# A four-layer graph network: attention scores as eight more columns of the dense product, a closed layer's bias and Relu on turned rows, and the zero fill told between its issues

## The reference, cut to what matters

```python
for l in range(3):
    h = (x @ W[l]).reshape(N, 4, 24)
    alpha_s = einsum('nhc,hc->nh', h, a_src[l])
    alpha_d = einsum('nhc,hc->nh', h, a_dst[l])
    e = leaky_relu(alpha_s[src] + alpha_d[dst], 0.2)
    ex = exp(e - segment_max(e, dst)[dst])
    alpha = ex / (segment_sum(ex, dst)[dst] + 1e-16)
    out = segment_sum(h[src] * alpha[:, :, None], dst)
    x = relu(out.reshape(N, 96) + b[l])
```

## Time and profile before

| | |
|---|---|
| timed runs | 12480.21 us median of 3 (12470.48 to 12484.04) |
| profiled execution | 12461.23 us, span 12459.3 us |
| busy share of the span | PE 49%, DVE 41%, ACT 33%, POOL 63% |
| chain that ended last | POOL 60%, issue 21%, PE 10%, DVE 5% |
| mean granted TensorE clock | 0.641 of full speed |

### The profile page before, as it was taken

How to read it: one execution, slowest core, us unless ns; L and a number is a source line. 1 busy time by engine, 2 the same in 40 slices (tenths; PEclk the granted TensorE clock), 3 DMA queues, 4 the chain that set the end, 5 groups by cost and what they waited for, 6 DMA issues and landing times.

```text
span 12459.3 us, 138299 instructions
## 1 busy us (share of the span) xinstructions
PE 6083.9 (49%) x36087; PEld 5305.1 (43%) x36087; DVE 5101.1 (41%) x15841; ACT 4053.9 (33%) x10426; POOL 7908.1 (63%) x8254
## 2 busy tenths in 40 slices
PE   0288721345555567998344444434343443434443
PEld 0188621234444446776333333434343343433343
DVE  8555400032332233223444444544444454444445
ACT  0199400034444440000333333233333323333332
POOL 1877777557777750000677777567777756777775
PEclk8556765666666668999555555555555555555555
DMA  8144421122222215665222222222222222222222
GB/s 281 24 103 102 134 73 42 55 50 53 53 53 53 53 36 160 215 214 189 69 69 67 68 67 68 53 69 69 67 68 67 68 53 70 68 67 68 67 69 59
DMA packets 1052646, 1038.35 MB, mean 83 GB/s; under 512 B 641642, under 2 KB 758166, under 8 KB 1051952
## 3 DMA queue, kind: packets, MB, share of 16 engines
q1 hardware_dynamic: 704544, 611.05, 16.7%
q0 software_dynamic: 263776, 336.86, 12.3%
q10 hardware_dynamic: 83664, 82.78, 2.0%
HBM read 935.12 MB, written 96.55 MB: 83 GB/s over the span
## 4 chain that ended last, share of the span: by engine, by line
POOL 60%; issue 21%; PE 10%; DVE 5%; ACTq 2%; DMA 1%; ACT 1%; DVEq 0%; POOLq 0%; SPq 0%; PEldq 0%
POOL sb_HG L571 47%; POOL edge_counts L624 13%; PE sums L968 3%; ACTq L642 2%; PE sums L905 1%; PE psA L968 1%; PE psB L968 1%; PE psC L968 1%; PE psD L968 1%; DVE sb_ACC L1939 1%; DMA edge_counts<-sb_HG 0%; PE psD L889 0%; DMA sb_HG<-attention_table,sb_NOW 0%; ACT sb_H L685 0%; PE psA L856 0%
## 5 line engine op out<-in xcount | busy, mean ns | idle before, releaser
L571 POOL DMA_INDIRECT sb_HG<-attention_table,sb_NOW x4980 | 4725.5, 949 | 3087.1 <-DVE sb_NOW L1768 1570.6
L905 PE MATMUL sums<-sb_HG 128*128 128x100 f32 x9984 | 2061.0, 398 | 444.2 <-ACT sb_HG L689 427.1
L905 PEld LDWEIGHTS sums<-sb_HG 128*128 128x128 f32 x9984 | 2028.1, 312 | 454.2 <-ACT sb_HG L689 436.1
L624 POOL DMA_INDIRECT edge_counts<-sb_HG x1625 | 1632.1, 1004 | 743.3 <-issue 489.2
L685 ACT ACTIVATE sb_H<-sb_iota_row,sb_H 128x128 f32<-128x128 f32 x6656 | 2029.1, 387 | 140.3 <-PE sums L905 65.7
L571 POOL DMA_INDIRECT sb_HG<-feature_table,sb_NOW x1612 | 1522.0, 944 | 641.8 <-issue 490.8
L1939 DVE TENSOR_TENSOR sb_ACC<-sb_ACC,sums 128x100 f32 x4992 | 1274.9, 255 | 1146.4 <-PE sums L905 618.9
L915 PEld LDWEIGHTS sums<-sb_HG 128*128 128x128 f32 x6656 | 1300.2, 294 | 345.9 <-issue 345.7
L915 PE MATMUL sums<-sb_HG 128*128 x6656 | 1314.9, 379 | 175.8 <-DVE sb_ACC L1485 80.7
L754 ACT ACTIVATE psC<-sb_SB 128x128 f32<-128x128 f32 x156 | 43.8, 281 | 3922.5 <-DVE sb_SB L1892 3922.5
L1485 DVE TENSOR_TENSOR sb_ACC<-sb_ACC,sums 128x97 f32 (+1 forms) x3328 | 848.7, 255 | 606.2 <-PE sums L915 124.6
(11 more groups left out here) (447 smaller groups left out, 8859.8 us busy)
## 6 DMA issues: line engine op xcount, KB each, us to landing
sb_HG<-edge_counts SPq DMA_DIRECT2D x1152, 256.0 KB, 3.2
sb_H<-rel_rows SPq DMA_DIRECT2D x312, 512.0 KB
sb_HG<-attention_table,sb_NOW POOLq DMA_INDIRECT x4980
sb_HG<-in_edge_attr_dram SPq DMA_DIRECT2D x201, 384.0 KB, 3.6
edge_counts<-sb_LW ACTq DMA_DIRECT2D x12, 6272.0 KB, 42.4
edge_counts<-sb_HG POOLq DMA_INDIRECT x1625
sb_HG<-feature_table,sb_NOW POOLq DMA_INDIRECT x1612, 2.4
sb_EA<-in_edge_attr_dram SPq DMA_DIRECT2D x201, 128.0 KB, 2.5
```

The costliest lines, as they stand in the source:

```text
L571: pool.indirect_dma_start(to, None, rows, bass.IndirectOffsetOnAxis(ap=index, axis=0)).then_inc(landed, 16)
L624: pool.indirect_dma_start(every_count, bass.IndirectOffsetOnAxis(ap=slot_of[:, f:f + 1], axis=0), tally[:, f:f + 1], None).then_inc(scatte ...
L905: last = nc.tensor.matmul(bank[:, k // 4, k % 4 * width:(k % 4 + 1) * width], HOT[:, hot, k, :], G[:, slot, k, 0:width], start=True, stop= ...
```

## The change

Three things change.

1. The fills. ScalarE waits for the fill two back, and tells it, between one issue and the next, instead of telling all after the last issue.
2. The scores. A product of h with a fixed vector is x times a column: W[:, head] times that vector. VectorE makes these columns once in the setup, 4 for the source and 4 for the target, behind each layer's weights in a new tile `WG` of 104 columns. The dense product is then 104 columns wide and gives features and both scores at once. `attend_to` becomes two copies: 100 columns into `ACC` and 4 into `DD`.
3. The close of layers 0 and 1. The division by the sum of weights moves into the next `gat` stage as `prepare` (`divide`, one group at a time, in `ACC`). TensorE turns `ACC` instead of `H`. ScalarE's lift adds the bias, now one value a partition, and rectifies. The last layer's close stays, behind the loop.

```diff
-            for g in [NG - 1, *range(NG - 1)]:
+            FILL = [NG - 1, *range(NG - 1)]
+            def tell_filled(n):
+                act.wait_ge(zeroed[FILL[n]], 16)
+                act.sem_inc(filled, 1)
+            for n, g in enumerate(FILL):
                 width = WIDE if g < NG - 1 else 2 * P
                 act.dma_start(counts[g, :, 0:NB, 0:width],
                               zeros[:, 0:width].unsqueeze(1).broadcast_to([P, NB, width])).then_inc(zeroed[g], 16)
-            for g in [NG - 1, *range(NG - 1)]:
-                act.wait_ge(zeroed[g], 16)
-                act.sem_inc(filled, 1)
+                if n >= 2:
+                    tell_filled(n - 2)
+            tell_filled(NG - 2)
+            tell_filled(NG - 1)
...
-            def lift(t):
+            def lift(t, bias=None):
+                how = {} if bias is None else {"bias": BCOL[:, bias:bias + 1]}
...
-                    nc.scalar.activation(zT[0:D, half, :], psA[0:D, :], ACT.Copy).then_inc(SEM["lifted"], 1)
+                    nc.scalar.activation(zT[0:D, half, :], psA[0:D, :], ACT.Copy if bias is None else ACT.Relu, **how)\
+                      .then_inc(SEM["lifted"], 1)
...
-                lift(Stage(f"gat{l}"))
+                lift(Stage(f"gat{l}"), bias=2 + l if l else None)
...
-                dense_stage(Stage(f"gat{l}"), H, W_GAT + l)
+                dense_stage(Stage(f"gat{l}"), ACC if l else H, WG[:, l, :], WT + HEADS)
...
+            dve.wait_ge(weights_in, (8 + P // DE) * 16)
+            for l in range(LAYERS):
+                for n, r in enumerate((R_ASRC, R_ADST)):
+                    link(v.tensor_tensor(SB[0:D, 0:D], WG[:, l, 0:D], ROWS[0:D, r + l, :], ALU.mult))
+                    link(v.tensor_reduce(WG[:, l, D + n * HEADS:D + (n + 1) * HEADS],
+                                         SB[0:D, 0:D].rearrange("p (h c) -> p h c", h=HEADS), AX.X, ALU.add))
             normalise()
...
-                    dve.wait_ge(SEM["taken"], g + score.base["taken"])
-                    v.tensor_copy(ACC[:, part, 0:D], p)
-                    for n, r in enumerate((R_ASRC, R_ADST)):
-                        last = v.tensor_tensor(by_head[n], p, row(r + l).broadcast_to([P, Q, D]), ALU.mult)
-                    last.then_inc(SEM["scored"], 1)
-                    dve.wait_ge(SEM["scored"], g + (score.base["scored"] + 1))
-                    for n, to in enumerate((ACC[:, part, D:WT], DD[:, part, :])):
-                        last = v.tensor_reduce(to, by_head[n].rearrange("p b (h c) -> p b h c", h=HEADS), AX.X, ALU.add)
-                    return last
-                take(score, attend_to)
+                    v.tensor_copy(ACC[:, part, :], p[:, :, 0:WT])
+                    return v.tensor_copy(DD[:, part, :], p[:, :, WT:WT + HEADS])
+                def divide(g):
+                    part = ACC[:, Q * g:Q * g + Q, 0:D].rearrange("p b (h c) -> p b h c", h=HEADS)
+                    by = ACC[:, Q * g:Q * g + Q, D:WT].unsqueeze(3).broadcast_to([P, Q, HEADS, C])
+                    return v.tensor_tensor(part, part, by, ALU.mult)
+                take(score, attend_to, prepare=divide if l else None, width=WT + HEADS)
...
                 link(v.reciprocal(ACC[:, :, D:WT], ACC[:, :, D:WT]))
-                for h in range(HEADS):
-                    part = ACC[:, :, h * C:(h + 1) * C]
-                    link(v.tensor_tensor(part, part, ACC[:, :, D + h:D + h + 1].broadcast_to([P, NBP, C]), ALU.mult))
-                link(v.tensor_tensor(ACCF, ACCF, over_blocks(row(R_GATB + l)), ALU.add))
-                if l < LAYERS - 1:
-                    link(v.tensor_scalar(H[:, :, :], ACCF, 0.0, None, ALU.max))
+            for h in range(HEADS):
+                part = ACC[:, :, h * C:(h + 1) * C]
+                link(v.tensor_tensor(part, part, ACC[:, :, D + h:D + h + 1].broadcast_to([P, NBP, C]), ALU.mult))
+            link(v.tensor_tensor(ACCF, ACCF, over_blocks(row(R_GATB + LAYERS - 1)), ALU.add))
```

More of the change, by code:

```diff
@@ L133, in gnn_kernel @@
         ones = sb("ones", [P, P])
-        WTS = sb("WTS", [D, 14, D])
+        WTS = sb("WTS", [D, 11, D])
+        WG = sb("WG", [D, LAYERS, WT + HEADS])
         WE = sb("WE", [P, P // DE, D])
         ROWS = sb("ROWS", [P, 7 + 4 * LAYERS, D])
-        BCOL = sb("BCOL", [D, 3])
+        BCOL = sb("BCOL", [D, 3 + LAYERS - 1])
         DD = sb("DD", [P, NBP, HEADS])
@@ L236, in gnn_kernel @@
         W_L0A, W_L0B, W_L0C, W_L0D, W_L11, W_L12, W_IN, W_GCN, W_OUT = 0, 1, 2, 3, 4, 5, 6, 7, 10
-        W_GAT = 11
         TURNED = [W_IN, W_GCN, W_GCN + 1, W_GCN + 2, W_OUT]
@@ L275, in gnn_kernel @@
                  "virtual_made",
-                 "prepared", "flipped", "lifted", "hid_product", "hid_ready", "made", "taken", "scored", "hop_step", "part_step"]
+                 "prepared", "flipped", "lifted", "hid_product", "hid_ready", "made", "taken", "hop_step", "part_step"]
         NAMES += [f"strip_in{n}" for n in range(RING)]
@@ L308, in gnn_kernel @@
             "dense": dense,
-            "scores": dense | {"scored": NG},
             "hop": dense | {"hop_step": 2 * NG},
@@ L321, in gnn_kernel @@
         for l in range(LAYERS):
-            PLAN += [(f"gat{l}", "scores"), (f"attend{l}", "attend")]
+            PLAN += [(f"gat{l}", "dense"), (f"attend{l}", "attend")]
         STORED = [16] + [16 + 16 * NG * (n + 1) for n in range(LAYERS)]
@@ L402, in _ @@
                 sp.dma_start(BCOL[:, 2:3], L1_b1.rearrange("(d a) -> d a", a=1)).then_inc(const_in, 16)
+                sp.dma_start(BCOL[:, 3:3 + LAYERS - 1], L3_bias[0:LAYERS - 1, :].rearrange("l d -> d l")).then_inc(const_in, 16)
             sp.dma_start(WTS[:, W_L0A:W_L0B + 1, :], L0_W1.rearrange("k (q n) -> k q n", q=2)).then_inc(weights_in, 16)
@@ L409, in _ @@
             sp.dma_start(WTS[:, W_OUT, :], L2_W_out).then_inc(weights_in, 16)
-            sp.dma_start(WTS[:, W_GAT:W_GAT + LAYERS, :], L3_W.rearrange("l a b -> a l b")).then_inc(weights_in, 16)
+            sp.dma_start(WG[:, :, 0:D], L3_W.rearrange("l a b -> a l b")).then_inc(weights_in, 16)
             for r in range(P // DE):
@@ L707, in _ @@
             act.dma_start(cols_now, src_cols).then_inc(cols_in, 16)
-            act.wait_ge(const_in, 14 * 16)
+            act.wait_ge(const_in, 15 * 16)
             lift_mlp(Stage("L0mlp"), 2, 0)
@@ L857, in flip_blocks, with dense_stage @@
                 last.then_inc(SEM["flipped"], 1)
-            def dense_stage(t, z, w):
+            def dense_stage(t, z, weights, width=D):
                 def product(g, half):
@@ L865, in product @@
                     for q in range(Q):
-                        last = nc.tensor.matmul((psD, psC)[half][:, q * D:(q + 1) * D],
-                                                zT[0:D, half, q * P:(q + 1) * P], WTS[:, w, :], start=True, stop=True)
+                        last = nc.tensor.matmul((psD, psC)[half][:, q * width:(q + 1) * width],
+                                                zT[0:D, half, q * P:(q + 1) * P], weights, start=True, stop=True)
                     last.then_inc(SEM["made"], 1)
@@ L1051, in _ @@
                                  start=True, stop=True).then_inc(feature_totals, 1)
-            dense_stage(Stage("in"), H, W_IN)
+            dense_stage(Stage("in"), H, WTS[:, W_IN, :])
             for l in range(LAYERS):
-                dense_stage(Stage(f"gcn{l}"), H, W_GCN + l)
+                dense_stage(Stage(f"gcn{l}"), H, WTS[:, W_GCN + l, :])
                 pe.wait_ge(SEM["taken"], Stage(f"gcn{l}").end["taken"])
@@ L1058, in _ @@
                 pe.wait_ge(SEM["sums_taken"], Stage(f"gcnsum{l}").end["sums_taken"])
-            dense_stage(Stage("out"), H, W_OUT)
+            dense_stage(Stage("out"), H, WTS[:, W_OUT, :])
             for l in range(LAYERS):
-                dense_stage(Stage(f"gat{l}"), H, W_GAT + l)
+                dense_stage(Stage(f"gat{l}"), ACC if l else H, WG[:, l, :], WT + HEADS)
                 t2 = Stage(f"attend{l}")
@@ L1469, in _ @@
             dve.wait_ge(x_in, 32)
-            dve.wait_ge(const_in, 14 * 16)
+            dve.wait_ge(const_in, 15 * 16)
+            dve.wait_ge(weights_in, (8 + P // DE) * 16)
[4 more added lines that the diff above has]
+                                         SB[0:D, 0:D].rearrange("p (h c) -> p h c", h=HEADS), AX.X, ALU.add))
             normalise()
@@ L1488, in add_up, with take @@
                     dve.wait_ge(SEM["acc_step"], U * g + (t.base["acc_step"] + k + 1))
-            def take(t, use, banks=(psD, psC), prepare=None):
+            def take(t, use, banks=(psD, psC), prepare=None, width=D):
                 def use_group(g, half):
                     dve.wait_ge(SEM["made"], g + (t.base["made"] + 1))
-                    use(g, banks[half][:, 0:Q * D].rearrange("p (b d) -> p b d", b=Q)).then_inc(SEM["taken"], 1)
+                    use(g, banks[half][:, 0:Q * width].rearrange("p (b d) -> p b d", b=Q)).then_inc(SEM["taken"], 1)
                 def prepare_group(g):
```

(15 more changed lines are left out.)

## The result

Before 12480.06 us (median; 12470.48 to 12484.04), after 12364.46 us (median of three; 12350.02 to 12365.72), a ratio of 0.9907 with the 95% interval [0.9889, 0.9924]. A fourth execution of the kernel after took 19270 us, for a reason that no trace shows, and is left out. The profiled execution took 12365.7 us, its span 12363.9.

A forecast was written before the change was run, and what follows sets the result against it. The prediction took POOL's serial indirect transfers as the bound, with VectorE pacing the score stages. Setup 47 plus stages 65 make 112 us off, 12461.2 to 12349; with the carried 19, 12368, range 12350 to 12390.

The forecast's parts named there:

- the 19 that I carried along: Profiled execution before lay 19 us under the timed median; that distance was added to 12349, giving 12368.
- Setup, 47 us: Setup: telling fills between issues starts POOL's first scatter at 205.8 instead of 252.78; gain 47, bounds nothing and 48.
- Fills two back cost no wait: ScalarE's fill loop: a fill lands 42.4 us after issue, 5.4 us into the issue then running, so nothing is held.
- the slower rival: Setup fills: waits between issues string the fills out, holding POOL's thirteenth partition; 12484 or 12622 us; chance 0.05.
- The rule against it: Setup: VectorE's port lock may hold the moved scatters; the row beside a counting pass, 0.96 us, says it doesn't.
- the rival of held scatters: Setup: VectorE's counting passes stretch scatters to 2.0 for 1.26 a step, losing 17 us; 12385; chance 0.07.
- Scores, 13.0 a layer, 39 in all: Score stages: fewer VectorE instructions let them run like `in`; gat0 takes 25.9 for 38.9 us, gaining 13.0.
- Close, 13.1 a layer, 26 in all: Layers 0 and 1: 14.26 us of VectorE passes go out, one 0.55 us product comes in; Relu with bias costs 0.7.
- The stages as a whole: gat0 25.9 us; 27.1 from the reciprocals' end to the end of gat1, and as much at gat2.
- SP's stores: Score stages: stores keep a 1.39 us step at no cost; as a rival they set the stage, 12404, chance 0.06.
- Low clock throughout: Score stages: eight steps of 2.50 instead of 1.39 us cost 8.9 a stage, 27 in all; 12395; chance 0.12.

The follow-up runs named there:

- the repeat: The changed kernel unaltered, run again beside seven executions of the kernel before: 12349.99 us, ratio 0.9902.
- the serial run: The changed kernel with each fill told right behind its own issue, so the next is issued only when it has landed: 12354.16 us, ratio 0.9905.

## Why the prediction was right

The time came 3.5 us from the forecast, 12364.46 for 12368, and its mechanisms are the ones that the runs show. That the distance is so small is partly luck: the scores gained 6 us more than priced, the close 3 to 5 less and the setup 2 less, and the 16.5 us that `L1mlp` cost in this profile nearly cancel the 19 that I carried along from the profile of before. The gain itself is the better test: forecast 112; 112 between the two profiles with `L1mlp` taken alike, 116 between the medians (interval 95 to 139).

- **Setup, 47 us:** 44.8 in the profile, 44.3 in the run with the fill alone, of which POOL kept 44.6 and 45.5. Of the 2.2 missing, 1.75 lie ahead of `fill_due`: VectorE's chain began 0.6 us later, when its first input had landed, and its last wait for TensorE had grown by 1 us (the transposes came 0.21 us apart until 195.1, in before until 192.4, and 0.11 from there on). The other 0.4 is SP's fetch: I allowed 2.1 us from `fill_due` to the first scatter, and it is 2.5. Shifts of that size lie between the runs in any case: with the new loop the first scatter is at 205.8 to 210.8.
- **Fills two back cost no wait:** right, and with more room than I knew. I took 42.4 us as the price of a landing; 22 of it was the other fills. The thirteenth partition was ready at 456.7 and not 435, and the last fill was down at 284.1. The worry of the slower rival, that scatters weigh on the fills, has something to it: the last two issues, which now run beside scatters, last 20.4 and 21.0 us for 18.5.
- **The rule against it:** of the 35 scatters between 206 and 252 us all but the first (1.19) lasted 0.95 to 0.97, on counting passes of 1.87 us: the row of before decided rightly, and the rival of held scatters is refuted. Under two-input products scatters are held, now as before; the Trainium skill, "SBUF — State Buffer", section "Who interferes with whom", infers that these leave the writing of descriptors alone, and the 7.53 us above differ from that.
- **Scores, 13.0 a layer, 39 in all:** 45 by themselves (12.5, 16.1, 16.8). The term I mis-sized is the number of low-clock steps: I took `in`'s five for all three stages, and the second and third had fewer. The wider product cost less than I allowed, too: 1.88 us for 1.86 at the low clock, 0.02 a step and not 0.15.
- **Close, 13.1 a layer, 26 in all:** 21 by itself, and 11.6 and 11.8 a layer on top of the short stage (37.2 us from reciprocals to cast of gat1 in the run with the scores alone, 25.5 in the changed kernel). Relu with bias is 0.68 for 0.59 as priced. Part of the rest is the clock: gat1 has three products at 0.50 in the profile after and two in the run with the scores alone, and a step costs 1.04 more there (2.52 for 1.48).
- **The stages as a whole:** 25.4, 25.5 and 24.7 us for the 25.9 and 27.1 forecast. The two errors above have opposite signs.
- **Adding up:** 48 + 46 + 21 = 115 us by the three parts alone; the change made 116 in its own comparison and 120 in the repeat. With intervals of 12 to 17 us on each part that shows no more than that they add up roughly; by the traces the close is worth 11.2 a layer by itself and 11.6 to 11.8 on top of the scores.
- **SP's stores:** thirteen in 19.85 us, no bound. **Low clock throughout** did not happen in a score stage. It happened in `L1mlp`, a place that the prediction did not look at: its forecast for the profiled execution, 12349, was 16.7 low, and 16.5 of that was lost there. The 19 us that I carried on to the median did not come again as a distance between profile and median (in the kernel after the profiled execution lies 1 us above it); that the clock of this stage is what they stand for is likely from the profile of before, and not shown.

## What to carry to other kernels

Take an instruction's cost on a busy engine from what a step grows by (0.28 us here for a duration of 0.55), and a transfer's landing from a row in which it is alone (20.0 for 43.0). Ask of an issue that lasts long whether it works or is held by what is under way ahead of it. And before a small gain is read from two profiles, compare the granted clock in stages that the change doesn't touch.

## What the runs showed of the hardware

- The dense stage `L1mlp`, in which TensorE's records leave hardly a gap (17.2 us busy of the first 18), stayed at 1.2 GHz for all its 61 us in four profiles and rose after 18, 32, 36 or 50 us in four others, with the same instructions. With twelve transposes in the pause of 4 us ahead of it and one more a step, three profiles had it at 2.4 GHz from 5 us into the stage on. The bursts that ended 1.5 to 5.4 us before a stage were all followed by a stretch at 0.50 of 3 to 17 us; the two that ended 1 us before the stage's beginning, or in it, kept it at 1.00.
- An indirect scatter of POOL that starts beside a VectorE product of two SBUF operands lasts beyond the product's end: 7.53 us under one of 7.09, for 0.96 without. Under a one-input f32 pass of 1.03 us one took 1.80 (profile after, at 331.87). Beside passes that write an accumulator scatters keep 0.95 to 0.97. Between 455 and 620 us of the serial run the long ones cost POOL 37 us.
- The issue of a 6.3 MB fill on ScalarE's queue lasts 18.5 us while two such fills are under way; with the one before it landed, the same issue takes 0.38.
